# Where the values stand in TensorE's order: whole or in halves, and a v projection in one job or two

## What is computed

```python
x = x + _layernorm(attn(_layernorm(x), Wq, Wk, Wv, Wo))
x = x + _layernorm(_layernorm(x) @ ternary(weight).T * alpha + bias)

def attn(x, Wq, Wk, Wv, Wo):            # B, S, D = 8, 1024, 256
    q, k, v = rope(x @ Wq), rope(x @ Wk), x @ Wv
    # each of the 4 k and v heads serves 4 query heads
    p = softmax(einsum('bhqd,bhkd->bhqk', q, k) / sqrt(256.))
    return einsum('bhqk,bhkd->bhqd', p, v) ... @ Wo
```

## Time and profile before

| | |
|---|---|
| median of 3 runs | 1704.89 us |
| the profiled execution | 1706.93 us, its span 1705.0 us |
| mean granted TensorE clock | 0.953 of full |
| busy: PE, DVE, ACT, POOL | 88%, 81%, 72%, 38% of the span |

### The profile page before, as it was taken

The page is one execution under the profiler, slowest core; times in us unless marked ns, Lnnn a source line. Parts: engine busy times, 40 slices in busy tenths (PEclk is TensorE's granted clock), DMA queues, the critical chain, the costliest instruction groups (busy, mean ns, idle before and its releaser), DMA issues.

```text
span 1705.0 us, 41144 instructions
## 1 busy us (share of the span) xinstructions
PE 1494.1 (88%) x13810; PEld 521.7 (31%) x13810; DVE 1389.6 (81%) x1899; ACT 1230.1 (72%) x2357; POOL 642.6 (38%) x703
## 2 busy tenths in 40 slices
PE   4589998989989899998999989998999998889872
PEld 3123233333333233332333323332333322222222
DVE  3697899878998789978898879977899789999914
ACT  1067888767877678777787768776788778878770
POOL 2121442454334443344425544254434354323230
PEclk8579999999999899999999999998999999999996
DMA  2311311113120320213111131202202121111010
GB/s 93 89 42 28 93 37 57 27 41 87 43 63 12 93 58 19 64 29 103 32 49 39 40 87 43 60 14 86 63 22 62 28 77 36 49 33 34 20 42 16
DMA packets 72805, 85.65 MB, mean 50 GB/s; under 512 B 17552, under 2 KB 58384, under 8 KB 71056
## 3 DMA queue, kind: packets, MB, share of 16 engines
q1 hardware_dynamic: 72592, 82.86, 17.3%
HBM read 46.66 MB, written 24.64 MB: 42 GB/s over the span
## 4 chain that ended last, share of the span: by engine, by line
PE 46%; DVE 31%; issue 12%; DMA 4%; POOL 3%; ACT 3%; SPq 1%; DVEq 0%; ACTq 0%; POOLq 0%
DVE row_max L1033 23%; PE pv L848 15%; PE smax L826 14%; PE ring L929 4%; PE ring L910 3%; PE ring L937 3%; PE ring L870 2%; DMA sums<-heads 2%; PE ring L916 2%; ACT heads L777 2%; DMA out<-res 1%; DVE sy_bn L1016 1%; ACT probs L734 1%; POOL res L442 1%; DVE sf_bn L1016 1%
## 5 line engine op out<-in xcount | busy, mean ns | idle before, releaser
L1033 DVE TENSOR_REDUCE row_max<-smax 128x1 f32<-128x1024 f32 x1024 | 1196.5, 1213 | 205.1 <-PE smax L826 203.9
L734 ACT ACTIVATE probs<-ring 128x512 f32<-128x512 f32 x2048 | 1098.8, 597 | 177.8 <-PE ring L870 159.5
L826 PE MATMUL smax<-k_rows,q_rows 48*128 48x512 f16 x2048 | 638.4, 393 | 107.5 <-DVE row_max L1033 89.8
L848 PE MATMUL pv<-probs,v_cols 128*32 128x256 f32 x8192 | 667.1, 398 | 33.4 <-ACT heads L777 33.0
L870 PE MATMUL ring<-q_rows,k_rows 50*128 50x512 f16 x2048 | 637.7, 389 | 0.1
L826 PEld LDWEIGHTS smax<-k_rows,q_rows 48*128 48x128 f16 x2048 | 128.8, 94 | 552.3 <-DVE row_max L1033 399.8
L848 PEld LDWEIGHTS pv<-probs,v_cols 128*32 128x32 f32 x8192 | 163.4, 108 | 429.4 <-issue 305.7
L870 PEld LDWEIGHTS ring<-q_rows,k_rows 50*128 50x128 f16 x2048 | 148.5, 94 | 37.3 <-ACT probs L734 15.7
L453 POOL TENSOR_TENSOR attnT<-pairs,inv_rows 128x512 f32<-128x512 f32 x31 | 39.5, 1273 | 276.0 <-DMA inv_rows<-inv_sums_dram 246.1
L436 POOL TENSOR_TENSOR act<-act,bias_sb 128x256 f32<-128x256 f32 x60 | 42.4, 728 | 118.6 <-ACT act L768 118.6
L721 ACT ACTIVATE rot_in<-ring 128x512 f32<-128x512 f32 x40 | 23.9, 597 | 83.8 <-PE ring L910 71.3
(11 more groups left out here) (130 smaller groups left out, 1024.2 us busy)
## 6 DMA issues: line engine op xcount, KB each, us to landing
q_stage_dram<-q_parts SPq DMA_DIRECT2D x48, 256.0 KB, 2.5
q_rows<-q_stage_dram SPq DMA_DIRECT2D x32, 384.0 KB, 5.6
x_in<-in_L_attn_x SPq DMA_DIRECT2D x8, 1024.0 KB, 5.9
pairs<-heads SPq DMA_DIRECT2D x64, 128.0 KB
inv_rows<-inv_sums_dram SPq DMA_DIRECT2D x32, 256.0 KB
res<-in_L_attn_x SPq DMA_DIRECT2D x16, 512.0 KB, 4.5
out<-res SPq DMA_DIRECT2D x16, 512.0 KB, 3.1
k_rows<-k_stage_dram SPq DMA_DIRECT2D x64, 96.0 KB, 3.3
```

Of the source, the lines that this page charges most:

```text
L734: eng.activation(probs[:, s % PSLOTS, j, :], ring[:, n % RING, :], ACT.Exp, scale=score_unit).then_inc(ring_read, 1)
L826: mm = eng.matmul(smax[:, side, c, :], q_rows[at:to, qc, kv * KVP + jp, qt * P:(qt + 1) * P], k_rows[at:to, kv, c * 512:(c + 1) * 512], st ...
L848: mm = eng.matmul(pv[j * VCOLS:(j + 1) * VCOLS, cols], v_cols[:, g, kt, :], probs[:, s % PSLOTS, j, cols], start=(kt == 0 and part == 0), ...
L1033: eng.tensor_reduce(row_max[:, g % 2, at:at + 1], smax[:, side, :, :].rearrange("p c n -> p (c n)"), AX.X, ALU.max).then_inc(max_read, 1)
```

## The change

In steps with a job other than `MT`, the values are issued whole (all 512 queries) behind the second pair (`i` 1). In the other even steps they are issued whole behind the third pair (`i` 2), in the other odd steps in two halves behind the second and fourth as before. The `V` projection becomes two jobs of 4 x 2 matmuls, in steps 20 and 21, each with its own slot of `ring` and its own move by ACT.

```diff
+ALL = (0, 2)
 PRO = {11: [("XT", 0, 0), ("XT", 1, 0)], 12: [("XT", 0, 1), ("XT", 1, 1)],
-       13: [("K",)], 17: [("Q", 0, 0)], 18: [("Q", 0, 1)], 20: [("V",)]}
+       13: [("K",)], 17: [("Q", 0, 0)], 18: [("Q", 0, 1)], 20: [("V", 0)], 21: [("V", 1)]}
...
+    def values_at(self, s):
+
+        if any(job[0] != "MT" for job in self.jobs(s)):
+            return {1: ALL}
+        return {2: ALL} if s % 2 == 0 else {1: (0, 1), 3: (1, 2)}
...
-                        eng.wait_ge(ring_read, h.done("V"))
+                        eng.wait_ge(ring_read, h.done("V", 1))
...
-                            move(v_next[:, :, :].rearrange("p t n -> p (t n)"), src)
+                            move(v_next[:, a[0] * ST:(a[0] + 1) * ST, :].rearrange("p t n -> p (t n)"),
+                                 src[:, 0:ST * HKV * HD])
...
-            def values(h, s, part):
+            def values(h, s, first, last):
...
-                cols = slice(part * HALF // 2, (part + 1) * HALF // 2)
+                cols = slice(first * HALF // 2, last * HALF // 2)
                 for j in range(G):
                     mm = eng.matmul(pv[j * VCOLS:(j + 1) * VCOLS, cols], v_cols[:, g, kt, :],
-                                    probs[:, s % PSLOTS, j, cols], start=(kt == 0 and part == 0),
+                                    probs[:, s % PSLOTS, j, cols], start=(kt == 0 and first == 0),
...
+                    parts = h.values_at(s) if (h.scores and s >= LAG) or (h.flush and s < LAG) else {}
...
-                        if i % 2 and ((h.scores and s >= LAG) or (h.flush and s < LAG)):
-                            values(h, s - LAG, i // 2)
+                        if i in parts:
+                            values(h, s - LAG, *parts[i])
...
-                            for t in range(KT):
+                            for t in range(ST):
                                 for dt in range(DT):
+                                    at = (a[0] * ST + t) * P
```

More of the change, by code:

```diff
@@ L830, in maxima @@
                     mm.then_inc(max_full, 1)
-            def values(h, s, part):
+            def values(h, s, first, last):
                 step = h.group0 * KT + s
                 g, kt = s // KT % HKV, s % KT
-                if part == 0:
+                if first == 0:
                     if kt == 0:
@@ L845, in values @@
                         eng.wait_ge(ring_read, h.base)
-                cols = slice(part * HALF // 2, (part + 1) * HALF // 2)
+                cols = slice(first * HALF // 2, last * HALF // 2)
                 for j in range(G):
                     mm = eng.matmul(pv[j * VCOLS:(j + 1) * VCOLS, cols], v_cols[:, g, kt, :],
-                                    probs[:, s % PSLOTS, j, cols], start=(kt == 0 and part == 0),
-                                    stop=(kt == KT - 1),
-                                    skip_group_check=True)
-                if part == 1:
+                                    probs[:, s % PSLOTS, j, cols], start=(kt == 0 and first == 0),
+                                    stop=(kt == KT - 1), skip_group_check=True)
+                if last == 2:
                     mm.then_inc(pv_step, 1)
@@ L913, in half @@
                         elif kind == "V":
-                            for t in range(KT):
+                            for t in range(ST):
                                 for dt in range(DT):
+                                    at = (a[0] * ST + t) * P
                                     mm = eng.matmul(dst[:, t * HKV * HD:(t + 1) * HKV * HD],
-                                                    xT[:, dt, t * P:(t + 1) * P], wv_sb[:, dt, :],
+                                                    xT[:, dt, at:at + P], wv_sb[:, dt, :],
                                                     start=(dt == 0), stop=(dt == DT - 1))
```

## The result

The kernel after takes 1808.72 us (median of 4 runs, 1805.95 to 1816.85) against 1704.1 us for the kernel before beside it: a ratio of 1.061, 95% interval 1.0585 to 1.0635. The forecast was 1729 with a range up to 1755. The sign was right, the size wrong: +104 us in place of +24. The profiled execution took 1805.95 us, its span is 1804.2.

The account below looks back on a forecast made before the run. PE and DVE bound each other: DVE just ahead in bare steps, PE in job steps. Two halves sum to +3.7 us, eight such +30, clock -6: +24; 1706.93 + 24 - 2 = 1729 us, range 1698 to 1755.

Parts of the forecast that it names:

- the coupling through `smax`'s one buffer a side: PE may start the third pair only when DVE has finished side 0 of the step before.
- part (1): Even steps without a job, values whole behind the third pair: 24 of 64 steps, losses of 7.9 us before credits.
- 7.9 - 1.3 - 0.3: Two halves' even steps: 7.9 us lost, less 1.3 not reaching PE-led next steps, less 0.3 hidden in step 28's stall.
- 3.00 us from side 0 to side 0: Bare even steps, DVE the bound: side 0's reduce starts no sooner than 3.00 us after its last; now 2.26.
- the upper end 1.14: Whole values to next pair at twice the half, 1.14 us not 1.00: adds 27 us, giving 1756.
- Job steps, -0.14 each: Whole values behind the second pair in 19 job steps of two halves save 0.14 us each: -2.7 us.
- 1.28 + 0.31 + 1.00 + 0.41: DVE-bound even steps: buffer free, pair to values, whole values, fourth pair to reduce; 3.00 us between side 0's reduces.
- 2 x 0.23 + 0.31 + 1.00: Even steps led by PE: fourth pair comes 1.77 us after the step's start in place of 1.33.
- the credits of -1.6 a pass: Even-step loss not passed on: -1.3 us where PE leads the next step, about 0.3 in step 28's stall.
- The fall at step 28: `qc` 0, clock drop after PE's 1.96 us pause, five of seven passes, mean 1.1 us: taken as gone, -6 us.
- rival C: More clock falls from PE's new pauses: ten more low stretches of 1 to 2 us each, 1750 us; chance 0.13.
- V in two jobs at about nothing: V projection split over steps 20 and 21: one more change of shape, +0.14 us for two halves.

Follow-up runs that it names:

- the short reduces: Each `row_max` reduce over 512 of its 1024 columns: 1614.31 us (0.9462) on the kernel before, 1608.02 us (0.9426) on the changed kernel.
- the two other places: Changed kernel with even steps' whole values behind the second pair, 1740.82 us (1.0203), or behind the fourth, 1740.42 us (1.0208), against the kernel before.

## Why the prediction was right in sign and wrong in size

- **What bounds, and the coupling through `smax`'s one buffer a side: right.** Shown by the rows above and by the short reduces, where the loss vanishes, and by the two other places, which remove two thirds of it.
- **The step that failed: part (1), the price of the even steps.** 7.9 - 1.3 - 0.3 a pass made 50 us; alone they cost 115. That is 65 of the 80 us missed. The floor was right, and what was wrong is what happens around it: the terms have DVE as the only one who can hold a third pair, they let a loss end with its step or credit 0.33 of it back, and they price every step at the full clock. The runs show third pairs held by ring slots, losses handed on (4-5 of `qc` 1), and 119 us more at the low level with the even steps alone. The fastest passes came to 11.4 us and not 6.3, and the clock and the jump to the rest, about 24 us.
- **3.00 us from side 0 to side 0: measured 3.09 in the loop and 3.01 behind it.** Whole values at 1.00 was right and the upper end 1.14 was not needed. Pair to values at 0.31 was right behind the loop (0.32); in the loop it is 0.40. Only about half of the 24 steps stand at this floor, so the lag is a small part of the miss.
- **Job steps, -0.14 each: right** in steps 8, 9, 24, 25. **Wrong where `MT` and a projection share the step** (5, 13, and with the V split 21): the prediction checked what DVE and PE do when the half values leave the place between fourth pair and jobs, and not that they were ACT's time to empty a slot. The pairs 12-13 and 20-21 of `qc` 0 came out 1.3 us a pass above the prediction. Pair 4-5 of `qc` 1 came out 0.46 above it, but the even steps alone do that too. And only eleven of the others gave the full 0.14. Alone, the job steps gave 8 us and not 21.
- **Third pair behind a job: wrong.** Both "1.28 + 0.31 + 1.00 + 0.41" and "2 x 0.23 + 0.31 + 1.00" know no wait for a slot. The third pair's score matmul needs one, and behind a job ACT holds it: pair 14-15 of `qc` 0 came out at +0.84, not +0.40, and 20-21 of `qc` 1 at +0.74, not +0.33. With the even steps alone it is +0.84 and +0.65.
- **What is left of the order of the work.** Of the 4.9 us a pass, the `MT` steps of `qc` 0 (1.3) and the pairs behind a job (0.85) are explained. Pairs 30-31 (`qc` 0) and 0-1 (`qc` 1) are 0.9 above the prediction together and are not explained; others are below it (2-3 and 18-19 of `qc` 1, 16-17 of `qc` 0), and the credits of -1.6 a pass can't be read apart in them. One cause was seen with the short reduces: a reduce that comes later is passed on where long DVE work follows, in steps that were put down as not bound by it.
- **The clock: wrong in sign.** The fall at step 28 was taken as gone, -6 us, since the pause ahead of it would shrink. It did, from 1.96 to 1.38 us, and the clock still fell in five of seven passes. A row of after:

```profile
604.21 0.60 PE L834 MATMUL smax<-k_rows,q_rows 48*128 48x512 f16 x1 [1.38 <-DVE row_max L1042]
```

  And new falls came in steps 12-13 and 18-19 of `qc` 1. This is rival C, at 0.13, as a part of the loss and not in place of the rest: 13 more stretches at the low level where it reckoned with ten, 66 us in all, and a drop in steps 18 and 19 costs 1.6 or 2.8 us. The argument against it was a comparison with one long pause; here several shorter ones come close together.
- **The loop's jump** was no term at all. The way over it grew by 1.8 us, from 12.37 to 14.20 on the mean of five. But 1.3 of that is there in the sixth pass too, which has no jump (7.70 to 9.03), and is counted in the 8.6. The jump itself took 0.5 us more, 2.5 in all.
- **V in two jobs at about nothing: right**, alone. Beside whole values it makes step 21 one more place with `MT` and a projection.
- **The sum.** Order of the work 8.6 us and not 3.7 a pass, 39 us in eight; clock and jump +3.1 and not -0.8, 31 us. Both miss in the same direction, and the upper end of the range held only the price of whole values, the term that came out exact.

## What to carry to other kernels

Before a block of work is moved on an engine that leads and follows in turn, list for each resource it passes (here `smax` and DVE, but also `ring` and ACT) what the block gave time to at its old place and what it delays at its new one: a burst inside the filling of a single buffer adds its whole length to the loop of waits. Merging two bursts in one saves turns of the engine only where nothing else turns with it, and the pauses that it leaves cost clock besides. In a kernel with a loop, compare versions by the fastest pass of each step as well as by the total, since code position alone moved the total of one kernel by 1.2%. Look which passes lie outside the loop: their fastest steps can hide what the loop does in every pass.

## What was not expected of the hardware

- Behind a wait for DVE, the `ring` matmul starts 0.08 us behind its `smax` partner in the code inside the loop (514.85, 514.93) and within 0.01 in the same code behind the loop (1476.66, 1476.67).
- With nearly the same pauses and the same work the clock fell in five of six halves inside the loop and stayed in one: 7.53 or 8.80 against 5.97 us for two steps. Values behind the fourth pair left the fastest passes as they were (193.12 against 193.30) and the kernel was 2.1% slower, by the clock and the jump.
- PE idles 3.35 and 4.38 us in the loop's jump for no other engine, with a transfer of an `instruction` queue at the start of the pause. In one kernel the way over the jump follows where the code stands: 10.86, 12.79 and 14.67 us for the same order with 12, 18 and 30 matmuls at the start. In the kernel before it does not.
